# Transposing six of the units of x while the first strip of the second weight is dequantised

## The reference

```python
cond = einsum('bsi,oi->bso', x, weight) + bias + scale[b] * (x @ A[b].T) @ B[b].T   # one adapter per batch
w    = NF4[codes] * absmax per block of 64
out  = x + einsum('bsd,od->bso', cond, w) + bias2
```

## Time and profile before

| | us |
|---|---|
| median of three runs | 2300.09 (2298.8 to 2300.9) |
| profiled execution | 2299.26 |
| its span | 2297.5 |
| TensorE busy | 2202.1 (96%) |
| VectorE busy | 1707.1 (74%) |
| ScalarE busy | 1116.0 (49%) |

### The profile page before, as it was taken

One profiled execution on the slowest core, in us unless ns is written; L12 is line 12 of the kernel. 1 busy time (PEld: TensorE's weight loads), 2 busy tenths in 40 slices (PEclk: granted clock), 3 DMA queues, 4 the chain that ended last, 5 costly groups with the idle time before them and its releaser, 6 DMA issues.

```text
span 2297.5 us, 37544 instructions
## 1 busy us (share of the span) xinstructions
PE 2202.1 (96%) x15082; PEld 2009.1 (87%) x15082; DVE 1707.1 (74%) x2434; ACT 1116.0 (49%) x1494; POOL 0.2 (0%) x4
## 2 busy tenths in 40 slices
PE   1489999999999999999999999999999999999999
PEld 1368877887788777899999999999999999999999
DVE  8988897897888565487777776676776676767665
ACT  6666665665666333354444443433444343443432
POOL 0000000000000000000000000000000000000000
PEclk9799999999999999999999999999999999999999
DMA  5248887887787898877777877777887777977775
GB/s 116 73 147 259 253 272 217 269 253 229 252 262 244 252 302 271 262 244 236 241 234 233 273 266 244 239 239 248 283 265 239 238 243 244 303 249 235 242 244 171
DMA packets 399331, 550.51 MB, mean 240 GB/s; under 512 B 41624, under 2 KB 256280, under 8 KB 399032
## 3 DMA queue, kind: packets, MB, share of 16 engines
q1 hardware_dynamic: 399160, 548.12, 76.0%
HBM read 421.66 MB, written 127.42 MB: 239 GB/s over the span
## 4 chain that ended last, share of the span: by engine, by line
PE 57%; DVE 0%; issue 0%; DVEq 0%
PE ps L1078 18%; PE ps L1076 18%; PE ps L1077 18%; PE ps L1119 1%; PE ps L1108 0%; DVE xs L870 0%; DVE res L949 0%; DVE res L927 0%; DVE res L942 0%; DVE low_st L887 0%; DVE low_rep L934 0%; DVEq L947 0%
## 5 line engine op out<-in xcount | busy, mean ns | idle before, releaser
L1076 PE MATMUL ps<-comb,xs 128*128 128x256 f32 (+1 forms) x3584 | 1014.6, 283 | 1.7 <-issue 1.0
L1078 PE MATMUL ps<-comb,xs 128*128 128x256 f32 (+1 forms) x3584 | 1014.6, 283 | 0.0
L1077 PE MATMUL ps<-comb,xs 128*128 128x256 f32 (+1 forms) x3584 | 1009.3, 282 | 0.0
L611 ACT CAST xs<-xr 128x1024 fp32r<-128x1024 f32 x427 | 448.1, 1051 | 633.2 <-DMA xr<-xc_d 632.7
L870 DVE TENSOR_TENSOR xs<-xr,xs 128x1024 fp32r<-128x1024 f32 x427 | 522.3, 1224 | 293.6 <-ACT xs L611 291.7
L1077 PEld LDWEIGHTS ps<-comb,xs 128*128 128x128 f32 x3584 | 677.8, 189 | 5.3
L1076 PEld LDWEIGHTS ps<-comb,xs 128*128 128x128 f32 x3584 | 676.6, 189 | 2.3 <-issue 1.4
L1078 PEld LDWEIGHTS ps<-comb,xs 128*128 128x128 f32 x3584 | 676.7, 189 | 0.0
L1076 PE MATMUL ps<-wq,tile 128*128 128x512 f32 x1088 | 476.1, 438 | 0.0
L1078 PE MATMUL ps<-wq,tile 128*128 128x512 f32 x1088 | 427.7, 393 | 0.0
L1077 PE MATMUL ps<-wq,tile 128*128 128x512 f32 x1088 | 426.7, 392 | 0.0
(11 more groups left out here) (99 smaller groups left out, 1720.2 us busy)
## 6 DMA issues: line engine op xcount, KB each, us to landing
xr<-xc_d SPq DMA_DIRECT2D x427, 512.0 KB, 4.0
raw<-in_L_cond_weight_dram SPq DMA_DIRECT2D x128, 512.0 KB, 4.6
xc_d<-rq SPq DMA_DIRECT2D x32, 1792.0 KB, 7.6
x_nat<-in_x_dram SPq DMA_DIRECT2D x128, 256.0 KB, 3.8
res<-in_x_dram SPq DMA_DIRECT2D x64, 512.0 KB, 5.4
out_dram<-res SPq DMA_DIRECT2D x128, 256.0 KB, 5.0
wc_d<-cs SPq DMA_DIRECT2D x32, 896.0 KB, 4.6
comb_raw<-wc_d SPq DMA_DIRECT2D x28, 1024.0 KB, 7.4
```

The source lines that it names most:

```text
L611: nc.scalar.copy(xs[f][:, HI, :, :], xr[f][:, LO, :, :]).then_inc(s_xhi, 1)
L1076: nc.tensor.matmul(out_ap, t_hi, m_hi, start=first, stop=False)
L1077: nc.tensor.matmul(out_ap, t_hi, m_lo, start=False, stop=False)
L1078: return nc.tensor.matmul(out_ap, t_lo, m_hi, start=False, stop=last)
```

## The change

Six units (24 groups, `EARLY = 6`) are transposed in the start-up. `EARLY_GROUPS` says how many groups go with each of the 16 pieces (2 with pieces 1 to 5, none with 6 and 7, 1 with 8 and 9, 2 with 10 to 15). TensorE transposes them ahead of the piece's own transposes, and ScalarE copies them at the end of its step for the piece, into `x_early`, five buffers of 8 KB per partition that lie where the second strip's weights come later. SP loads the groups in the same loop and stores each finished unit's four blocks to their fields in `xc_d`. The sums of these units stay in jobs 2m + 2 and 2m + 3: SP loads the four blocks back into `rq` at the start of the even job, once the previous unit's sums have been stored, VectorE's sums wait for it, and only the four fields that the sums change are stored. Jobs 1 to 12 have no transposes of x any more. SP's order in the start-up is rewritten for this: three x groups are loaded ahead of the adapters, and in each later step the codes come first, then x groups, then a finished unit's store, then the adapters' columns or tile halves.

```diff
+    EARLY_OF = [2, 3, 0, 1]
+    EARLY_GROUPS = [0, 2, 2, 2, 2, 2, 0, 0, 1, 1, 2, 2, 2, 2, 2, 2]
+    EARLY = sum(EARLY_GROUPS) // 4
+    BEFORE_A = sum(EARLY_GROUPS[:6])
...
-        return [2 * g - 2] if g % 2 else [2 * g - 3, 2 * g - 2, 2 * g - 1]
+        return [i for i in ([2 * g - 2] if g % 2 else [2 * g - 3, 2 * g - 2, 2 * g - 1]) if i >= 4 * EARLY]
...
+        x_early = [at(f"x_early{i}", 88 + 8 * i, [P, 4, QK, P], F32) for i in range(5)]
...
             def store_x_sums(m):
                 p, c = divmod(m, 2)
+                f = slice(S2, A22) if m < EARLY else slice(0, NF)
                 sp.wait_ge(s_sums, 4 * (m + 1))
-                sp.dma_start(xc_d[p, :, :, c * QK:(c + 1) * QK, :].rearrange("f p k t -> p f k t"),
-                             rq[:, :, :, :]).then_inc(s_xst, 16)
+                sp.dma_start(xc_d[p, f, :, c * QK:(c + 1) * QK, :].rearrange("f p k t -> p f k t"),
+                             rq[:, f, :, :]).then_inc(s_xst, 16)
+
+            def store_early(m):
+                p, c = divmod(m, 2)
+                sp.wait_ge(s_xcp, 4 * (m + 1))
+                for u, f in ((slice(0, 2), slice(A11, S2)), (slice(2, 4), slice(S3, NF, 2))):
+                    sp.dma_start(xc_d[p, f, :, c * QK:(c + 1) * QK, :].rearrange("f p k t -> p f k t"),
+                                 x_early[m % 5][:, u, :, :]).then_inc(s_early[m % 5], 16)
+
+            def load_early(m):
+                p, c = divmod(m, 2)
+                sp.wait_ge(s_early[m % 5], 32 * (m // 5 + 1))
+                if m:
+                    sp.wait_ge(s_xst, 16 * m)
+                for f in (slice(A11, S2), slice(S3, NF, 2)):
+                    sp.dma_start(rq[:, f, :, :], xc_d[p, f, :, c * QK:(c + 1) * QK, :].rearrange("f p k t -> p f k t")
+                                 ).then_inc(s_back, 16)
...
+            load_groups(3)
             sp.dma_start(a_nat[:, :], lora_a.rearrange("a r i -> (a r) i")).then_inc(s_a_nat, 16)
             for n in range(2, 6):
                 load_codes(n)
+                load_groups(sum(EARLY_GROUPS[:n - 1]) + 3)
+                store_early_of(n - 3)
                 for a in (2 * n - 4, 2 * n - 3):
                     sp.dma_start(b_cols[:, a * R:(a + 1) * R], lora_b[a]).then_inc(s_bcols, 16)
...
+                if g % 2 == 0 and 0 <= (g - 2) // 2 < EARLY:
+                    load_early((g - 2) // 2)
...
                 if n == PIECES:
                     act.wait_ge(s_a_st, 16)
+                    for i in range(5):
+                        act.wait_ge(s_early[i], 32 * len(range(i, EARLY, 5)))
...
+                if m < EARLY:
+                    dst = x_early[m % 5][:, EARLY_OF[r], :, :]
+                    if r == 0 and m >= 5:
+                        act.wait_ge(s_early[m % 5], 32 * (m // 5))
+                else:
+                    dst = rq[:, GROUP_OF[r], :, :]
+                    if r == 0:
+                        act.wait_ge(s_xst, 16 * m)
...
+                for i in early_groups(n):
+                    copy_group(i)
...
             def x_sum(m, step):
                 a11, a12, s2, s1, a21, s4, a22 = (rq[:, f, :, :] for f in range(NF))
+                if m < EARLY:
+                    dve.wait_ge(s_back, 32 * (m + 1))
...
             def select_a():
                 pe.wait_ge(s_a_nat, 16)
+                pe.wait_ge(s_xcp, BEFORE_A)
...
             for n in range(PIECES):
+                for i in early_groups(n):
+                    for t in range(QK):
+                        transpose_x(i, t)
                 transpose_piece(n)
```

More of the change, by code:

```diff
@@ L115, in groups_of, with early_groups @@
             return []
-        return [2 * g - 2] if g % 2 else [2 * g - 3, 2 * g - 2, 2 * g - 1]
+        return [i for i in ([2 * g - 2] if g % 2 else [2 * g - 3, 2 * g - 2, 2 * g - 1]) if i >= 4 * EARLY]
+    def early_groups(n):
+        first = sum(EARLY_GROUPS[:n])
+        return range(first, first + EARLY_GROUPS[n])
     def group_at(i):
@@ L252, in adaln_ffn_kernel @@
         s_xcp = sem("x_group_copied")
+        s_early = [sem(f"early_x_blocks_stored{i}") for i in range(5)]
+        s_back = sem("early_x_blocks_loaded")
         s_sums = sem("x_sums_made")
@@ L325, in store_x_sums, with load_groups, store_early_of @@
                 p, c = divmod(m, 2)
+                f = slice(S2, A22) if m < EARLY else slice(0, NF)
                 sp.wait_ge(s_sums, 4 * (m + 1))
-                sp.dma_start(xc_d[p, :, :, c * QK:(c + 1) * QK, :].rearrange("f p k t -> p f k t"),
-                             rq[:, :, :, :]).then_inc(s_xst, 16)
+                sp.dma_start(xc_d[p, f, :, c * QK:(c + 1) * QK, :].rearrange("f p k t -> p f k t"),
[14 more added lines that the diff above has]
+                                 ).then_inc(s_back, 16)
+            loaded, stored = [0], [0]
+            def load_groups(stop):
+                while loaded[0] < min(stop, 4 * EARLY + 3):
+                    load_group(loaded[0])
+                    loaded[0] += 1
+            def store_early_of(n):
+                while 4 * (stored[0] + 1) <= sum(EARLY_GROUPS[:n + 1]):
+                    store_early(stored[0])
+                    stored[0] += 1
             def store_w_sums(j, k):
@@ L406, in _ @@
                 load_codes(n)
+                load_groups(sum(EARLY_GROUPS[:n - 1]) + 3)
+                store_early_of(n - 3)
                 for a in (2 * n - 4, 2 * n - 3):
                     sp.dma_start(b_cols[:, a * R:(a + 1) * R], lora_b[a]).then_inc(s_bcols, 16)
[L409 to L418, removed]
-                load_codes(n)
+            for n in range(6, PIECES):
+                load_codes(n)
+                load_groups(sum(EARLY_GROUPS[:n - 1]) + 3)
+                store_early_of(n - 3)
+                if n < 8:
+                    for h in range(2):
+                        load_half(n - 6, h)
                 if n == 10:
@@ L423, in _ @@
                                  a_raw[:, :, :, :, :].rearrange("p b h k r -> p b (h k r)")).then_inc(s_a_st, 16)
-            load_codes(PIECES)
-            load_codes(PIECES + 1)
+            for n in (PIECES, PIECES + 1):
+                load_codes(n)
+                load_groups(sum(EARLY_GROUPS[:n - 1]) + 3)
+                store_early_of(n - 3)
+            store_early_of(PIECES - 1)
             for g in range(JOBS):
@@ L590, in copy_group @@
                 act.wait_ge(s_tr, i + 1)
-                if r == 0 and m:
-                    act.wait_ge(s_xst, 16 * m)
-                nc.scalar.copy(rq[:, GROUP_OF[r], :, :], tr_x[i % 2][:, :].rearrange("p (t s) -> p t s", t=QK)
+                if m < EARLY:
[6 more added lines that the diff above has]
+                        act.wait_ge(s_xst, 16 * m)
+                nc.scalar.copy(dst, tr_x[i % 2][:, :].rearrange("p (t s) -> p t s", t=QK)
                                ).then_inc(s_xcp, 1)
@@ L984, in _ @@
                 j, s = divmod(g, S1)
-                n, groups = pieces_of(g), groups_of(g)
-                m = (g - 2) // 2
+                n, m = pieces_of(g), (g - 2) // 2
                 if s == 1:
@@ L997, in _ @@
                     dequantise_a(n)
-                if g % 2 and groups_of(g - 1):
+                if g % 2 and 3 <= g <= 2 * UNITS + 1:
                     x_sum((g - 3) // 2, 3)
@@ L1001, in _ @@
                     dequantise_b(n)
-                if g % 2 == 0 and groups:
+                if g % 2 == 0 and 2 <= g <= 2 * UNITS:
                     x_sum(m, 0)
@@ L1084, in transpose_x @@
                         pe.wait_ge(s_xcp, i - 1)
-                    else:
+                    if i in (BEFORE_A, BEFORE_A + 1):
                         pe.wait_ge(s_a_cp, 4)
```

## The result

The changed kernel takes 2291.57 us (median of 7 runs, 2290.71 to 2292.88), the kernel before 2299.99 beside it (7 runs, 2297.98 to 2300.9). The ratio is 0.9965, with a 95% interval from 0.9955 to 0.9975: 8.4 us faster, 0.37%. The forecast was 2290.0 with a range from 2285.5 to 2298.5.

What follows compares the result with a forecast made beforehand. TensorE was taken as the bound after a start-up set by VectorE's chain. 10.7 + 0.8 - 1.6 - 0.2 = 9.7 us off 2299.26 gives 2289.6, forecast as 2290.0 with about half of 0.8 added; range 2285.5 to 2298.5.

Steps and rivals of the forecast that it cites:

- The main loop: Jobs 1 to 12: 96 transposes leave TensorE, worth 12.0 us; VectorE becomes the bound, so 10.7 us gained.
- step (c): Start-up, piece 2: x loads ahead make codes 2.2 us late, with two ScalarE copies 1.6 us lost (bounds 0.8, 2.4).
- (a): Start-up, TensorE: 96 added transposes, eight per piece, fit in 5.8 us of air; cost 0.
- (b): Start-up, ScalarE: two copies per piece, 1.2 us, fit in its 2.3 us wait for VectorE; cost 0.
- (d): Start-up, later pieces: codes still land in time; cost 0, at most 1.5 us per piece whose load takes 8 us.
- step (e): Before the last piece: early transposes may prevent TensorE's half clock, 1.7 us gained or nothing; taken as 0.8 us.
- The blocks read back: Main loop, even jobs: VectorE's first sum waits for reloaded blocks, 1.9 us to spare; 0.2 us lost in all.
- Rival C: Main loop: waiting for blocks read back costs 2.5 us in five units, 2302.1 us; chance in full 0.14.
- Rival A: TensorE's full price gained, start-up not delayed, clock stays up: 13.7 us gained, 2285.6 us; chance 0.12.
- Rival B: Start-up: code loads behind x traffic land late in six pieces, 9 us lost, 2299 us; chance in full 0.11.

Runs made afterwards that it cites:

- experiment 4: Experiment 1's first kernel with one sum per early unit on GpSimd: 2292.52 us; experiment 5's matmul kernel with one VectorE step shortened: 136.33 us from tile 1 to 13.
- experiment 1: Changed kernel with three x loads behind piece 2's codes (first kernel): 2289.10 us; kernel before with its first three x loads ahead of the adapters: 2303.27 us.
- experiment 5: Experiment 1's first kernel with 12 matmuls or 22 transposes before piece 15's transposes: 2287.44, 2287.64 us; side by side, 2287.52 without and 2287.86 with transposes.
- experiment 3: Changed kernel with the two loads of a unit's blocks issued half a job later: 2321.77 us in one run.
- experiment 2: Experiment 1's first kernel with the bias load behind piece 2's codes, adapters behind piece 4's, adapters' columns spread over pieces 2 to 5: 2290.02 us.

## Why the prediction was right

Time and direction were right. The median came out 1.6 us above the forecast, and the sum itself was further off: 9.7 us of gain forecast, 6.9 measured, because one term was mis-sized and another gave nothing. By its steps, for the profiled pair:

- The main loop: forecast 10.7, measured 11.0. Both halves hold. A transpose costs 0.125 us by intervals and not its busy time (mean 286 ns after), and VectorE becomes the bound (experiment 4). The forecast pair was 23.03, against 22.93 measured at the end of the stretch. The bound cost 1.0 us, forecast 1.3.
- The start-up, step (c): forecast -1.6, measured -4.1. This is the term that was off. The mechanism was right (experiment 1), but the codes' lateness was taken as 2.2 us, between bounds of 1.4 and 3.0, and was 4.25 (4.55 less the 0.3 by which everything was late from the first codes on). With that, and 0.94 us for the two copies (24.64 to 25.58) instead of 1.2, the step's own sum gives 4.25 + 0.94 - 1.26 - 0.57 = 3.4 us, and piece 2 cost 3.3. No step had the other 0.8 us: 0.5 at piece 8 behind transposes at half clock, and 0.3 before the first piece, of which no run shows the cause. The bounds priced the issues and the bytes ahead of the codes, and left out the queue itself: the x loads took the place directly behind the element-wise bias load, 3.2 us for one issue, which the adapters' load had paid before, and everything behind came late and landed more slowly.
- Steps (a), (b) and (d), the rest of the start-up at no cost: right to within about 1 us; 0.2 us for 24 groups in the profile of experiment 1, from -0.6 to 1.6 in those of the kernels built on it.
- The clock, step (e): forecast +0.8 as half of 1.7, measured 0 in this pair. Both profiles have the half clock; the idle time before it was 3.08 us and not 2.5. By experiment 5 it differs between two profiles of the same kernel, by about 1.5 us, so no mean gain can be claimed.
- The blocks read back: forecast -0.2 with 1.9 us to spare, measured 0 with 1.4. Rival C is refuted for this change, its price per microsecond confirmed (experiment 3).
- Rival A needed a TensorE-bound pair; that is 22.73 us and was seen only in the first. Rival B's late codes came, at piece 2 alone, not in six pieces.

11.0 - 4.1 = 6.9 us of span, against 9.7 forecast. The medians are 8.4 us apart, since this profiled execution is 1.0 us slower than its kernel's median and the one before 0.7 us faster than its own. So the time was closer to the forecast than the sum by luck.

## What to carry to other kernels

Price work taken out of a busy TensorE stream by the intervals of what follows it, then ask at once which engine has less air than that: here VectorE had 1.65 us a pair where 2.0 were given. When a DMA is put into a queue in front of others, ask what stands ahead of it and what it pushes back, not only how many bytes it has: three loads of 256 KB in the wrong place cost 2.8 us, 24 in the right places 0.2, each in one profile. Compare more than one profile of the same code before a difference of 1 to 2 us is explained: the same start-up ended anywhere within 2.2 us here, and a gain of about 1.5 us seen between medians of four or five runs on different chips went away when the kernels ran side by side.

## What the runs showed of the hardware

- A GpSimd subtraction of 128x512 float32 took 2.08 us, and a VectorE sum of 128x256 that met it 1.40 us instead of 0.43 (experiment 4).
- One issue on SP took 3.2 us directly behind a load of 2048 single elements, whether it was a load of x (the changed kernel) or of the adapters (experiment 1's first kernel). Two loads of 128 KB in 64-byte pieces took 7.88 us to issue behind a load of 1 MB (experiment 2).
- After idle times of TensorE of 2.72 us (experiment 1's first kernel) and 3.07 us (the same kernel in experiment 5), the next matmuls ran at half clock in the first profile and at full clock in the second.
